# First attention of a four-layer graph network: a second pass of scores with keys along partitions, shifted by row minima laid as two more rows, in place of turning the probabilities

## The reference, cut to what matters

```
qkv = (x @ w_qkv).reshape(b, n, 3, H, hd).transpose(2, 0, 3, 1, 4)
q, k, v = (qkv[0], qkv[1], qkv[2])
attn = jnp.einsum('bhnd,bhmd->bhnm', q, k) * scale
attn = jnp.where(attn_mask[None, None] == 0, -jnp.inf, attn)
attn = jax.nn.softmax(attn, axis=-1)
o = jnp.einsum('bhnm,bhmd->bhnd', attn, v).transpose(0, 2, 1, 3).reshape(b, n, d)
```

## Time and profile before

| | |
|---|---|
| time, median of three executions | 2557.17 us (2555.69 to 2558.51) |
| span of the profiled execution, first to last instruction | 2555.1 us |
| PE busy | 2518.8 us (99%) |
| DVE busy | 1872.5 us (73%) |
| ACT busy | 1935.7 us (76%) |
| POOL busy | 757.7 us (30%) |

### The profile page before, as it was taken

How to read it: one execution, slowest core, us unless ns; L and a number is a source line. 1 busy time by engine, 2 the same in 40 slices (tenths; PEclk the granted TensorE clock), 3 DMA queues, 4 the chain that set the end, 5 groups by cost and what they waited for, 6 DMA issues and landing times.

```text
span 2555.1 us, 50270 instructions
## 1 busy us (share of the span) xinstructions
PE 2518.8 (99%) x17401; PEld 2043.1 (80%) x17401; DVE 1872.5 (73%) x5440; ACT 1935.7 (76%) x4388; POOL 757.7 (30%) x1083
## 2 busy tenths in 40 slices
PE   8999999999999999999999999999999999999997
PEld 6777787888878888888888888888888888778875
DVE  8858848778686786867768587685877868666776
ACT  5858849678596886959869597785968869675787
POOL 2223332323224232242332324232232322423222
PEclk9999999999999999999999999999999999999999
DMA  5302113022130312203122131221303123021122
GB/s 145 78 19 59 26 46 71 26 61 45 46 77 20 76 30 59 65 21 77 43 54 53 41 70 32 54 51 46 78 19 67 38 54 70 20 52 27 28 54 69
DMA packets 91083, 132.15 MB, mean 52 GB/s; under 512 B 15921, under 2 KB 40146, under 8 KB 90834
## 3 DMA queue, kind: packets, MB, share of 16 engines
q1 hardware_dynamic: 90834, 128.94, 21.4%
HBM read 19.83 MB, written 8.39 MB: 11 GB/s over the span
## 4 chain that ended last, share of the span: by engine, by line
PE 91%; ACT 3%; DVE 3%; issue 1%; SPq 1%; POOL 1%; DMA 0%; ACTq 0%; POOLq 0%; DVEq 0%
PE bank L1451 18%; PE bank L1453 18%; PE bank L1452 18%; PE bank L1508 16%; PE bank L1523 9%; PE bank L1500 8%; PE bank L1528 2%; PE bank L1491 2%; PE bank L1561 1%; ACT probs L990 1%; ACT PT L999 1%; DVE gate L1209 0%; ACT res L1027 0%; SPq L749 0%; DVE probs L1224 0%
## 5 line engine op out<-in xcount | busy, mean ns | idle before, releaser
L990 ACT ACTIVATE probs<-probs,few 128x512 f32<-128x512 f32 x1024 | 732.0, 722 | 38.9 <-DVE few L1224 36.5
L1224 DVE CUSTOM_DVE_ANT_0 probs<-bank,mask 128x512 f32<-128x512 f32 x1024 | 675.4, 685 | 111.8 <-PE bank L1508 65.2
L1508 PE MATMUL bank<-ident,probs 128*128 128x128 f32 x4096 | 580.5, 273 | 7.0 <-ACT probs L990 5.9
L1508 PEld LDWEIGHTS bank<-ident,probs 128*128 128x128 f32 x4096 | 485.4, 141 | 76.6 <-issue 10.3
L999 ACT ACTIVATE PT<-bank 128x512 f32<-128x512 f32 x672 | 377.7, 594 | 51.9 <-PE bank L1528 42.8
L1500 PE MATMUL bank<-stack 96*128 96x512 f32 x1024 | 411.6, 450 | 1.0 <-DVE few L1224 0.8
L1235 DVE COPY PT<-bank 128x512 f32<-128x512 f32 x352 | 240.7, 687 | 69.5 <-PE bank L1528 48.2
L1451 PE MATMUL bank<-feat,W 128*128 128x512 f32 x640 | 258.6, 404 | 0.0
L884 POOL TENSOR_TENSOR feat<-o,feat 128x256 fp32r<-128x256 f32 x128 | 95.2, 743 | 542.0 <-ACT feat L1012 541.5
L1453 PE MATMUL bank<-feat,W 128*128 128x512 f32 x640 | 252.7, 395 | 0.0
L1452 PE MATMUL bank<-feat,W 128*128 128x512 f32 x640 | 252.7, 395 | 0.0
(11 more groups left out here) (113 smaller groups left out, 4972.7 us busy)
## 6 DMA issues: line engine op xcount, KB each, us to landing
stack<-qk SPq DMA_DIRECT2D x768, 128.0 KB, 2.4
res<-in_x_dram SPq DMA_DIRECT2D x16, 512.0 KB, 3.8
out_dram<-res SPq DMA_DIRECT2D x16, 512.0 KB, 3.0
rows<-bo_sum SPq DMA_DIRECT2D x15, 128.0 KB, 2.9
rows<-in_L_gnn_bias_dram SPq DMA_DIRECT2D x14, 128.0 KB, 2.9
rows<-in_L_gnn_ln_beta_dram SPq DMA_DIRECT2D x14, 128.0 KB, 2.9
PT<-in_adj_dram SPq DMA_DIRECT2D x1, 1024.0 KB, 5.3
vh<-in_L_gnn_w_w_dram SPq DMA_DIRECT2D x2, 512.0 KB, 9.3
```

Source lines behind the costliest of these rows:

```text
L990: k = act.activation(p, p, ACT.Exp, bias=least[:, t % P_RING:t % P_RING + 1], scale=-1.0, accum_out=sums[:, grp % 2, q * HG + h:q * HG + h ...
L1224: k = dve.tensor_tensor_reduce(out=probs[:, t % P_RING, :], in0=place("scores", t)[:, :], in1=mask[:, half * QT + q, :], scale=1.0, scalar ...
L1508: k = pe.transpose(place("transpose", t)[:, m * P:(m + 1) * P], probs[:, t % P_RING, m * P:(m + 1) * P], ident[:, :])
```

## The change

In the first attention alone (layer 1) the probabilities are no longer turned. The scores are computed twice:

- The first pass (L1782, the same matmul as before) is only for the row minima: DVE (L1465) adds the mask and takes the minimum into `row_least`; its 512-wide output goes back into the same bank, and nobody reads it.
- After 16 tiles (two heads, SHIFTS = 2; a "side") one transpose (`least_rows`, L1791, PE) turns the minima, ACT (L1237) and DVE (L1481) write their negative as high and low half into `feat`, and four small transfers (L984, 8 pieces of 128 elements each) lay them as rows 96 and 97 under the stacked q. Rows 96 and 97 of k hold ones.
- The second pass, called st (`columns`, L1805, PE): 98 rows, keys as the stationary side: two matmuls of 128 keys by 256 queries into a bank. They hold the shifted scores, keys along partitions.
- `exp` (L1212, ACT) reads the bank and writes `PT`, with neither bias nor sum. `only_edges`, called mask (L1490, DVE), takes the minimum with 0 or 1 from adjT, so that keys without an edge give 0.
- `add_up`, called padd (L1115 once per head and half of a group, L1111 and L1113 for the second two pieces, POOL) adds PT up over the keys' tiles into `acc`; `edge_values` (L1821 and L1828, PE) multiplies PT with v in two parts of 8 matmuls, and then four matmuls of ones by `acc` give each head's row sums on its 32 rows. DVE takes the reciprocal of 128 by 256 sums (L1516) ahead of its multiplication (L1518).

The third layer's attention keeps its form. The order of blocks is now a list of units (half a block), some buffers hold two heads' stacks of the second group in `qk` itself ("own"), and RANK has other numbers.

```diff
+LATE |= {"st": 0.13, "mask": 0.11, "padd": 0.15, "minT": 0.28, "neg": 0.14, "neglo": 0.11, "negrow": 2.0, "onerow": 2.0}
...
-RANK = {"act a": 6.5, "act ax": 3, "act hT": 6.5, "act hf": -5.5, "act k": 0.5, "act n0": -8, "act n1": -4,
...
+RANK = {"act a": -1.06, "act c": 7.45, "act hT": 12.43, "act hf": 88.57, "act k": 1047.99, "act n1": 49.17,
...
+            def columns(t):
+                layer, b, g, half, *_ = tile_of(t)
+                i, h = in_columns(t)
+                wait_free(pe, "st", t)
+                if half == 0 and i == 0 and h % SHIFTS == 0:
+                    pe.wait_ge(shift_row[h // SHIFTS], (side_at[b, g, h // SHIFTS] + 1) * 16 * 2 * SHIFTS)
...
+                rs = slice(0, STACKED * HD + 2)
+                for c in range(2):
+                    m = 2 * i + c
+                    k = pe.matmul(place("st", t)[:, c * QH:(c + 1) * QH], side(layer, b, g, h, 1)[rs, m * P:(m + 1) * P],
+                                  side(layer, b, g, h, 0)[rs, half * QH:(half + 1) * QH], start=True, stop=True)
+                fill(k, "st", t)
...
+            def edge_values(grp, part):
...
+                pe.wait_ge(masked.sem, masked.at(grp * GROUP + (part + 1) * HG - 1))
+                for c in range(2):
+                    m = 2 * part + c
+                    for h in range(HG):
+                        at = (g * HG + h) * HD
+                        k = pe.matmul(dst[h * HD:(h + 1) * HD, 0:QH], v_v[j][:, m, at:at + HD],
+                                      PT[:, part * HG + h, c * QH:(c + 1) * QH], start=(m == 0), stop=(m == NT - 1))
+                if part == 0:
+                    half_read.raised_by(k, grp)
+                else:
+                    pe.wait_ge(added_up.sem, added_up.at((grp, HG - 1, 1)))
+                    for h in range(HG):
+                        k = pe.matmul(dst[h * HD:(h + 1) * HD, QH:2 * QH], one[:, 0:1].broadcast_to([P, HD]),
+                                      row_sums(b, g, h), start=True, stop=True)
...
+            def least_rows(b, g, hp):
...
+                k = pe.transpose(place(*name)[:, 0:P], before_ident[:, at:at + P], ident)
...
+                    k = dve.tensor_tensor_reduce(
+                        out=place("scores", t)[:, :], in0=place("scores", t)[:, :],
+                        in1=mask1[:, q, :], scale=1.0, scalar=3.4e38, op0=ALU.add, op1=ALU.min,
+                        accum_out=row_least[:, least_at(h, q):least_at(h, q) + 1])
...
+            def only_edges(t):
...
+                dve.wait_ge(exped1.sem, exped1.at(t))
+                p = PT[:, t % PT_RING, :].rearrange("p (m q) -> p m q", m=2)
+                k = dve.scalar_tensor_tensor(p, adjT[:, HI, 2 * i:2 * i + 2, half * QH:(half + 1) * QH].bitcast(F32), 0.0, p,
+                                             ALU.not_equal, ALU.min)
...
+                    m = mark(dve.reciprocal(o32[:, :], place("values", grp)[:, QH:2 * QH]))
...
+                    k = act.activation(PT[:, t % PT_RING, :], place("st", t)[:, :], ACT.Exp, scale=-1.0)
...
+            def add_up(grp, h, i):
...
+                if i:
+                    pool.wait_ge(added_up.sem, added_up.at((grp, h, 0)))
+                    added_up.raised_by(pool.tensor_tensor(to, to, first, ALU.add), (grp, h, "more"))
+                    pool.wait_ge(added_up.sem, added_up.at((grp, h, "more")))
+                    k = pool.tensor_tensor(to, to, second, ALU.add)
+                else:
+                    k = pool.tensor_tensor(to, first, second, ALU.add)
...
+                elif key[0] == "negrow":
...
+                    for s in (HI, LO):
+                        r = STACKED * HD + s
+                        for h in range(hp * SHIFTS, (hp + 1) * SHIFTS):
+                            i = h % SHIFTS * NT
+                            sp.dma_start(side(1, b, g, h, 0)[r:r + 1, :].bitcast(F32).rearrange("p (q n) -> p q n", q=NT),
+                                         shifts(b, g, hp, s)[i:i + NT, :].bitcast(F32)).then_inc(shift_row[hp], 16)
```

427 lines of the change are left out of this document (332 added, 95 removed), and 9 rows, old and new, of the table RANK.

## The result

The changed kernel takes 2836.64 us (median of 4 runs, 2835.30 to 2838.83) against 2556.48 for the kernel before on the same chip: a ratio of 1.110, with an interval of 1.108 to 1.111. It is 11% slower; the forecast was 2523 us, and its range ended at 2585.

What follows compares the result with a forecast made beforehand. PE's own instruction list was taken as the bound: 2555.1 us less 74 of PE work gives 2481, plus 40 of waiting 2521, plus 2.1 to the median 2523 us; range 2476 to 2585.

Steps and rivals of the forecast that it cites:

- the +20 in DVE's sum: Collisions of DVE's masks with POOL: 0.04 us on each of 512 masks, 20 us.
- the 40 us of new waiting on PE: PE's added waits: 15 us at the start, 10 + 15 for small waits and the shifts; ends 0 and 90.
- DVE's sum: DVE's predicted work: 1872.5 us with copies removed and masks, reciprocals, low halves and collisions added, 2192 us, 88% of 2481.
- my 1.53: DVE's reciprocal of 256 columns, estimated at 1.53 us from two rows of that engine; 64 of them, +86 us net.
- My upper end of 190 us: Upper bound for collisions on DVE: half a POOL operation, 0.37 us, on every mask, +190 us.
- rival 1: DVE becomes the bound through masks and reciprocals, deciding from about 2450 us of DVE work; 2580 us, chance 12%.
- rival 3: PE saves too little: second-pass tiles cost 0.32 us, steps in and out twice as much; 2561 us, chance 9%.
- the -74: Net change of PE's work from transposes, second pass, values with row sums, and minima: 74 us less.
- -228, +120, +25 and +9: PE's terms in us: transposes removed, second pass added, values and row sums, transposes of minima.
- rival 2: Shifts come late through SP's list or the landing, and PE waits for each of 64 sides; 2575 to 2636, chance 9%.
- cover of 6.5 us: PE's 24 products and 8 transposes between the minima's transpose and the first tile needing it: 6.5 us, no slack.
- the shifts' way: New path to exp: transpose, ACT, DVE, four issues on SP and landing, about 6.2 us.

Runs made afterwards that it cites:

- the run with both parts short: The changed kernel, lists kept, with masks over 16 of 512 columns and POOL's additions over 16 of 256; 2610.53 us, ratio 1.021.
- the two runs with short parts: The changed kernel, lists kept, with masks and additions cut to 16 columns, without and with reciprocals replaced by copies; 2610.53 and 2604.64 us.

## Why the prediction was wrong

**The step that failed is the collisions with POOL, the +20 in DVE's sum, where the trace has 300 us of holds, 146 of them on the masks.** A second one failed with it, the 40 us of new waiting on PE: the run with both parts short, at 2611 us, lies outside the forecast's range too. Without the +20 DVE's sum was 2172 us; the trace has 2464, of which 300 by the count above are holds, so the rest of the sum stood within 10 us, the reciprocal's 1.750 us against my 1.53 (+14) among it. I took the present mean of L1333 over its median, 23 ns, and scaled it by POOL's share. That was wrong twice. POOL's operations in the kernel before are seldom beside such an operation: the count finds a POOL operation running at 6 of L1333's 96 starts. Additions are released by masks, and masks stand in runs: additions fill 25% of the changed kernel's span, and 232 of 512 masks (45%) start beside one. Where one operation releases the other, a mean share is not the chance of meeting. And I priced only the masks. As much again (154 us) fell on untouched operations with two SBUF sources, which the row of L1333 itself pointed at, and 124 of the 300 us were beside operations that POOL had before, which I took for settled by the old order. My upper end of 190 us, half a POOL operation on every mask, was fair for the masks (146) and blind to those.

The rule cited there, from the Trainium skill (SBUF — State Buffer, section Who interferes with whom), says that the second to start is blocked until the first is through. The trace now agrees in size: over the 286 masks that start beside a POOL operation of 256 columns or more, the hold follows the time that the POOL operation had left, with a slope of 0.92 (correlation 0.94), 0.54 us where 0.6 to 0.8 was left. It needed no new rule, only its consequence for pairs that release each other.

**Second, rival 1 was the right mechanism and too cheap.** I let DVE decide from about 2450 us of work on, and put 50 us of idle time and 60 of lockstep behind it: 2473 + 110. DVE has 2464, and the time is 2837: it idles for 371 us. A tile of the first attention now goes through exp, mask, additions, sums, reciprocal and output on four engines with in-order lists, and a hold of 1 to 2 us anywhere can move all of them (argued from the lists; no run isolates it). DVE was at 87% of the span at most in any run, and at 89% in the middle of this one. The signs that I named for rival 1 (DVE over 2400, masks over 0.8 us, the chain over DVE) all came, and I had given it 12%.

**Third, PE's step was right and its waiting wasn't.** Starts of the second pass are 0.12 us apart, rival 3 is out:

```profile
1059.02 0.65 PE L1805 MATMUL bank<-stack 98*128 98x256 f32 x4
1059.50 0.40 PE L1805 MATMUL bank<-qk 98*128 98x256 f32 x2
1059.74 0.28 PE L1728 MATMUL bank<-W,feat 128*128 128x256 f32 x1
```

To check the -74 I took the starts of PE in ten samples of the run with both short, which has the changed kernel's lists. At the medians of their kinds, transposes cost 14.0 us a sample less, the second pass 7.7 more, values with sums 2.3 more, turned outputs 1.1 less, minima 0.5 more: -4.6 us a sample, x16 = -74. The kernel before takes 155.7 us a sample, so this should be 151.1. It takes 157.8 (2.1 more than before), so 6.7 us a sample are waits that the kernel before doesn't have, 107 us over the run. One sees them in the step from a scores matmul that stands behind another to whatever comes next: 0.231 us in the kernel before, by mean and median, and in this run a median of 0.233 with a mean of 0.269. The page hides most of it: over ten samples' time of that run it shows PE busy for 98.6%,

```profile
490.00:2047.00 1557.00, 1535.77 (x10319) 1205.98 (x10318) 1244.74 (x3639) 1023.65 (x2172) 546.42 (x1103) 1.00 0.22 51
```

because a matmul's row lasts 0.28 to 0.48 us where the next could start after 0.12 to 0.23, and a wait that ends within that counts as busy. My "40 us of new PE waiting" was an estimate from idle times, and idle times are blind below some 0.2 us. So even without collisions between masks and additions the change, with these lists, would have lost: -74 of work and +107 of waits make +33 of the 54 measured. Term by term, over 16 samples, that is -224 for the transposes, +123 for the second pass, +19 for values with sums and turned outputs and +8 for the minima, where I had put -228, +120, +25 and +9. The other 20 or so I put, by subtraction only, on the first and last samples: the first two take 17 us more than before in that run, and the granted clock there is 0.93 from 54 to 128 us and 0.89 from 128 to 256, where it was 1.00. What each of the small waits is for isn't settled, nor how many of them come from the 116 us of holds that this run still has. That they hardly shrink with DVE's load is shown (the two runs with short parts), and that another order alone can bring as many is shown for the kernel before (63 us).

**Fourth, rival 2 didn't come.** PE's waits at L1805 over the whole run are for ACT, issue and DVE, none for a transfer:

```profile
  ACT PT L1212: 10.4, 11
  issue: 8.2, 20
  DVE before_ident L1465: 5.1, 5
```

So the cover of 6.5 us was enough for the shifts' way, better than an estimate of that closeness deserved; the way's own length wasn't measured. At the start, where I had put 15 us, the first two samples lost 17 with both parts short and 66 with them whole.

Points that came out as said: ACT 1686 us against 1671; 2048 transposes left; starts 0.12 us apart. PE's idle time on the page is 240 us, not 60 to 90.

The order of the sizes, then: taking away either side of the meetings between masks and additions, with the lists kept, brings 175 or 193 of the 280 us. Shortening both brings 226, but that takes some 240 us of other DVE work away as well. The last 54 us stand against 74 that PE has less to issue; they are small waits whose causes are open.

## What to carry to other kernels

Before giving POOL elementwise work that starts when a DVE operation ends, count DVE's operations with two SBUF sources, all of them and not only the new ones, and price each at the chance that the two meet in the new order, not at POOL's mean share: here 45% of the masks met an addition, and old pairs that never met before met too. Put one source in PSUM or drop it, and the cost goes. Add holds to the engine's work before asking whether it becomes the bound. A busy share near 100% on PE is no proof that it doesn't wait: compare the time for one unit of work between two fixed marks, and, for matmuls behind the same kind of matmul, the mean of the start-to-start steps with the median. Where a planner with a tuned table lays out the lists, an experiment that adds or drops pieces measures the table; keep the lists and shorten the instruction, or tune again.

## What the runs showed of the hardware

- A DVE operation with both sources in SBUF waits for most or all of what a running POOL operation of 256 columns or more has left (slope 0.92 over 286 masks), also when the DVE operation needs 0.18 us itself (up to 2.13 us for 16 columns).
- Small POOL operations held nothing, though the profile shows them running for 0.2 to 1.2 us: 111 masks began beside operations of two columns at no cost, and all DVE operations that began beside additions of 16 columns lost 3 us together, in the run with only the additions short.
- A DVE operation with one source in a PSUM bank (the minimum with the mask added, the mask added in the bank, the multiplication into `o`) or a single source (reduction) showed no hold beside 580 us and more of additions.
- POOL pays too: a mean of 0.91 to 0.96 us for an addition of 128x256 beside the masks, 0.75 to 0.83 without them (median 0.74).
- A reciprocal of 256 float32 columns out of PSUM takes 1.750 us. The Trainium skill (VectorE: DVE Perf Modes, section Walkthrough: the 8-slice pipeline in each mode) gives it a repeat of 8; the estimate of 2.3 us made from that was too high, and my 1.53 from the row of the small reciprocal too low.
- An addition of 16 columns on POOL takes a median of 0.22 us where one of 256 takes 0.74. Beside whole masks its mean is 0.34 to 0.39 us, beside short ones 0.23 to 0.24.
